# A graph network's update stage: the second tile's normalised rows are turned one step later

## The reference

```python
h = h + (agg.reshape(n, TD) @ wo[l] + bo[l])
xn2 = _layernorm(h, ln2_g[l], ln2_b[l])
ffn = jax.nn.gelu(xn2 @ w1[l] + b1[l], approximate=False) @ w2[l] + b2[l]
h = h + ffn
```

```python
edge_proj = edge_attr @ W_sum + b_sum
sum3d = jax.ops.segment_sum(edge_proj, src, num_segments=num_nodes)
```

## Time and profile before

| | us |
|---|---|
| median of 3 runs | 5238.9 (5233.25 to 5239.08) |
| the profiled execution's own time | 5237.1 |
| its span in the trace | 5235.3 |
| PE busy | 3812.7 (73% of the span) |
| DVE busy | 3650.4 (70%) |
| ACT busy | 2132.3 (41%) |
| POOL busy | 3941.4 (75%) |
| first and last norm of update(0) | 1874.9 and 2516.5 |
| first and last norm of update(1) | 4223.3 and 4973.9 |

### The profile page before, as it was taken

The page is one execution under the profiler, slowest core; times in us unless marked ns, Lnnn a source line. Parts: engine busy times, 40 slices in busy tenths (PEclk is TensorE's granted clock), DMA queues, the critical chain, the costliest instruction groups (busy, mean ns, idle before and its releaser), DMA issues. The chain is left out here.

```text
span 5235.3 us, 86953 instructions
## 1 busy us (share of the span) xinstructions
PE 3812.7 (73%) x17590; PEld 3000.8 (57%) x17591; DVE 3650.4 (70%) x9882; ACT 2132.3 (41%) x5069; POOL 3941.4 (75%) x4715
## 2 busy tenths in 40 slices
PE   1695777777777778888685777777777767777759
PEld 0344555555555567778443555555555557766646
DVE  3696888888888856666474888888888844444458
ACT  0113555555555523333113555555555523333322
POOL 2217888888888647777787888888888658888867
PEclk9898999999999989998896999899999978888879
DMA  3366666667666556666676766677666456666658
GB/s 112 118 201 199 201 199 199 197 197 201 198 196 199 144 129 140 139 130 134 117 156 176 203 197 199 197 196 202 199 198 197 134 128 127 125 123 126 132 142 238
DMA packets 664282, 882.62 MB, mean 169 GB/s; under 512 B 126257, under 2 KB 492269, under 8 KB 664013
## 3 DMA queue, kind: packets, MB, share of 16 engines
q0 software_dynamic: 261248, 529.64, 42.8%
q1 hardware_dynamic: 369907, 322.55, 20.8%
q10 hardware_dynamic: 32860, 28.05, 1.9%
HBM read 749.33 MB, written 130.59 MB: 168 GB/s over the span
## 5 line engine op out<-in xcount | busy, mean ns | idle before, releaser
L859 POOL DMA_INDIRECT kv<-kv_scratch,src_u x1760 | 1687.4, 959 | 364.3 <-POOL spacer L839 189.4
L1130 PE MATMUL sum_p<-msg,hot_s 128*128 128x273 f32 x3520 | 1091.6, 458 | 736.5 <-issue 499.5
L1318 POOL DMA_INDIRECT sum_scratch<-ysum,dest x700 | 1100.9, 1573 | 284.1 <-issue 153.5
L1130 PEld LDWEIGHTS sum_p<-msg,hot_s 128*128 128x128 f32 x3520 | 716.7, 215 | 1024.5 <-issue 697.5
L1118 PE MATMUL qe<-sums,hot_q 128*128 x3520 | 900.6, 401 | 74.5 <-ACT hot_q L890 48.8
L1118 PEld LDWEIGHTS qe<-sums,hot_q 128*128 128x128 f32 x3520 | 715.5, 206 | 216.9 <-issue 84.6
L996 DVE SCALAR_TENSOR_TENSOR sums<-sums,keep,sum_p 128x273 f32 x880 | 434.6, 494 | 436.7 <-PE sum_p L1130 326.5
L899 ACT ACTIVATE hot_s<-iota_f,ndrel_u 128x128 f32<-128x128 f32 x1760 | 559.4, 391 | 307.2 <-PE sum_p L1130 209.5
L970 DVE TENSOR_TENSOR prod<-qe,kv 128x1024 f32<-128x1024 f32 x440 | 535.9, 1218 | 67.5 <-DMA kv<-kv_scratch,src_u 66.4
L839 POOL MEMSET spacer<- 128x384 bf16 x1320 | 573.9, 435 | 0.9
L985 DVE TENSOR_TENSOR msg<-kv,turned 128x1024 f32<-128x1024 f32 x440 | 533.1, 1212 | 44.3 <-issue 34.6
(11 more groups left out here) (247 smaller groups left out, 5237.7 us busy)
## 6 DMA issues: line engine op xcount, KB each, us to landing
drow<-drel_scratch SPq DMA_DIRECT2D x220, 256.0 KB
ea<-in_edge_attr SPq DMA_DIRECT2D x100, 512.0 KB
srow<-in_src_rows SPq DMA_DIRECT2D x100, 512.0 KB
kv<-kv_scratch,src_u POOLq DMA_INDIRECT x1760
kv_scratch<-res SPq DMA_DIRECT2D x100, 256.0 KB
hin<-h_scratch SPq DMA_DIRECT2D x154, 128.0 KB
h_scratch<-res SPq DMA_DIRECT2D x150, 128.0 KB
masks<-mask_scratch SPq DMA_DIRECT2D x110, 128.2 KB
```

What stands on the lines that cost most here:

```text
L859: g.indirect_dma_start(out=kv[:, slot, :], out_offset=None, in_=KVd, in_offset=bass.IndirectOffsetOnAxis(ap=src_u[:, par, u:u + 1], axis=0 ...
L1130: ins = pe.matmul(sum_p[i][:, 0:XW], hot_s[:, q % 2, 2 * i + u, :], msg[:, q % 2, 2 * i + u, :], start=(u == 0), stop=(u == 1))
L1318: g.indirect_dma_start(out=sum_d[r], out_offset=bass.IndirectOffsetOnAxis(ap=dest[:, k, j:j + 1], axis=0), in_=ysum[:, k, j, :], in_offset ...
```

## The change

The norm of the second tile (DVE), its transposes (TensorE) and its copy (ScalarE) leave the end of the turn. In the next turn norm(t, 1) stands behind attention(t + 1, 0), turn_norm(t, 1) behind up(t, 0), and turned_norm(t, 1) behind gelu(t, 0). The first tile's turn_norm(t + 1, 0) and turned_norm(t + 1, 0) change places with the att steps of the second tile, so they stand ahead of them. The steps ahead of the loop and behind it follow from that. POOL's and SyncE's lists are unchanged, and both calls of update() get the same change.

```diff
                        for k in range(2):
                            stats(0, k)
-                        for k in range(2):
-                            norm(0, k)
+                        norm(0, 0)
 
                         def turn(t):
                             attention(t + 1, 0)
+                            norm(t, 1)
                             repeats(t, 0)
                             result(t, 0)
                             stats(t + 1, 0)
...
                             result(t, 1)
                             stats(t + 1, 1)
                             next_moments(t, 1)
-                            norm(t + 1, 1)
 
                         with v.Fori(0, PAIRS - 1) as t:
                             turn(t)
+                        norm(PAIRS - 1, 1)
...
-                        for k in range(2):
-                            turned_norm(0, k)
+                        turned_norm(0, 0)
                         a.wait_ge(prep, 2)
                         with a.Fori(0, PAIRS - 1) as t:
                             gelu(t, 0)
+                            turned_norm(t, 1)
                             turned_att(t + 1, 0)
                             sums_out(t, 0)
                             gelu(t, 1)
+                            turned_norm(t + 1, 0)
                             turned_att(t + 1, 1)
-                            turned_norm(t + 1, 0)
                             sums_out(t, 1)
-                            turned_norm(t + 1, 1)
-                        for k in range(2):
-                            gelu(PAIRS - 1, k)
-                            sums_out(PAIRS - 1, k)
+                        gelu(PAIRS - 1, 0)
+                        turned_norm(PAIRS - 1, 1)
+                        sums_out(PAIRS - 1, 0)
+                        gelu(PAIRS - 1, 1)
+                        sums_out(PAIRS - 1, 1)
...
-                        for k in range(2):
-                            turn_norm(0, k)
+                        turn_norm(0, 0)
                         with pe.Fori(0, PAIRS - 1) as t:
                             up(t, 0)
+                            turn_norm(t, 1)
                             turn_att(t + 1, 0)
                             down(t, 0)
                             out_proj(t + 1, 0)
                             sum_group(t, 0)
                             up(t, 1)
+                            turn_norm(t + 1, 0)
                             turn_att(t + 1, 1)
-                            turn_norm(t + 1, 0)
                             down(t, 1)
                             out_proj(t + 1, 1)
                             sum_group(t, 1)
-                            turn_norm(t + 1, 1)
-                        for k in range(2):
-                            up(PAIRS - 1, k)
-                            down(PAIRS - 1, k)
-                            sum_group(PAIRS - 1, k)
+                        up(PAIRS - 1, 0)
+                        turn_norm(PAIRS - 1, 1)
+                        down(PAIRS - 1, 0)
+                        sum_group(PAIRS - 1, 0)
+                        up(PAIRS - 1, 1)
+                        down(PAIRS - 1, 1)
+                        sum_group(PAIRS - 1, 1)
```

## The result

The changed kernel takes 5251.7 us (median), the kernel before 5239.1 us in the runs beside it. The ratio is 1.0024, with a 95% interval of 1.0015 to 1.0033. So the change costs 12.7 us. That is slower by 0.24%, where 5232 us and a range of 5205 to 5251 us were forecast. Ten of the eleven executions of the changed kernel took 5247 to 5255 us; one took 9206 us, in a slower state of the chip, and stands outside the ratio.

A forecast was written before the change was run, and what follows sets the result against it. Update(0) was taken as bound by POOL's scatter loop and the edge-load loop, update(1) by POOL's queue. Saving 7 us in update(0) and 0 in update(1): 5237.1 - 7 + 1.8 = 5232 us, range 5205 to 5251 us.

The forecast's parts named there:

- what the change does on TensorE: TensorE, update(0): up(t, 0) starts without a wait; idle time moves to turn_norm(t + 1, 0), down(t, 1) behind it 2.0 us longer.
- What the second turn_norm was to keep, about 1 us: TensorE, update(0): idle time left at turn_norm(t, 1), waiting for xn behind up(t, 0), about 1 us.
- POOL is next: POOL, update(0): scatters colliding with loads limit the turn next; landing waits still 60 us or more.
- What is late next: POOL: Update(0): earlier loads collide with POOL's scatters, holding the turn at 26.4 us.
- POOL pays 2.2 us, and the turn is 24.2 + 2.2 = 26.4 us: POOL, update(0): second scatter 6.86 us behind the last one instead of 4.7 us without a wait.
- The saving of 7 us: Update(0): 24 turns at 26.4 us instead of 26.7 us save 7 us; update(1) saves 0.
- The other 2.5 us are mostly one wait: POOL, update(0): the turn's 2.5 us beyond 24.2 us are mostly the second tile's second scatter awaiting the first tile's sixth.
- The load loop is then 26.2 us, level with POOL's 26.3 us: Update(0): load loop of 24.2 us plus 2.0 us for a slow down(t, 1); both loops together give 26.4 us.
- rival (c): Nothing to measure: rs withholds what TensorE stops withholding, DVE's wait changes its name only; 5239 us, chance 0.22.
- rival (b): Update(0): load loop gets free of the collision and sets a 25.2 us turn; 36 us saved, 5203 us, chance 0.17.
- Rival (d): Update(1): cold down(t, 1) makes loads 2 us later, sixth to eighth scatters land late; 16 us slower, 5255 us, chance 0.16.
- DVE's waits for products under 20 us: Sign in update(0): DVE's waits for TensorE's products fall from 68 us to under 20 us.

The follow-up runs named there:

- a_warm: Changed kernel plus 20 filler transposes of the identity on TensorE ahead of turn_norm(t + 1, 0); 5252.3 us, ratio 1.0023 to the kernel before.
- a_rot: Changed kernel with the second tile's scatter tables in update(0) turned by two, (j + 2) % 4; 5211.4 us, ratio 0.9946 to the kernel before.
- b_rot: Kernel before the change with the second tile's scatter tables in update(0) turned by two; 5208.1 us, ratio 0.9934.
- a_loads: Changed kernel with each tile's store and edge loads right behind its own node loads on SyncE; 5273.5 us, ratio 1.0063 to the kernel before.
- a_again: The unedited changed kernel measured a second time; 5252.5 us, ratio 1.0023 to the kernel before.
- only_u1: Kernel before with the changed order in update(1) alone; 5243.7 us, ratio 1.0010.
- only_u0: Kernel before with the changed order in update(0) alone; 5249.6 us, ratio 1.0017.
- a_noswap: Changed kernel with turn_att(t + 1, 1) again ahead of turn_norm(t + 1, 0) on TensorE; 5255.6 us, ratio 1.0030 to the kernel before.
- late loads: Both stores issued ahead of the first edge load on SyncE: in the changed kernel 5235.1 us (0.9992), in the kernel before 5229.0 us (0.9978).
- the same filler: 20 extra transposes ahead of turn_norm(t + 1, 0): in the changed kernel 5252.3 us, in the changed kernel with tables turned by two 5203.5 us.

## Why the prediction was wrong

**Right: what the change does on TensorE.** up(t, 0) starts without a wait. The idle time went to the first tile's turn_norm, 3.11 us within the forecast 2 to 4 us, and made down(t, 1) 1.7 us longer (forecast 2.0 us). What the second turn_norm was to keep, about 1 us, went as well.

The Trainium skill (TensorE: Matmul & The Clock Gate, section HAM oscillation) says that in a loop of matmuls each batch behind a wait for its data starts cold, and the trace of the changed kernel agrees in its steady turns: behind each of the twelve waits of 3.10 to 3.12 us down took 4.5 to 5.3 us. It doesn't in one turn: behind the 3.38 us at 2025.69 us down took 3.62 us. The section gave no price for the kernel, and a_warm measured it: 0.6 us in the wrong direction, within the intervals, as long as POOL sets the turn.

**Right: POOL is next.** The landing waits stayed (68.9 us, at least 60 forecast). The turn hung on the collision of loads and scatters, and a_rot and b_rot show it by taking the waits behind it away.

**Wrong: the size of the collision.** The step that failed is in "What is late next: POOL": "POOL pays 2.2 us, and the turn is 24.2 + 2.2 = 26.4 us". The 2.2 us came from the one turn that began with xn waiting for rs, with a distance of 6.86 us at a place of -1.45 us. The 19 turns of a_warm with a place between -1.38 and -1.34 us average 7.3 us (6.8 to 7.9 us), so that turn was a lucky one. The old kernel's own mean was already 7.09 us, that is 2.4 us paid, and 24.2 + 2.4 = 26.6 us is no gain. The changed kernel's is 7.38 us: 2.7 us paid, 3.1 us in its steady turns. With that, 24.2 + 2.7 = 26.9 us, against 27.0 us measured; this only shows that the sum closes, since the 2.7 us were measured afterwards. The saving of 7 us was the difference of a lucky turn and an average.

The place of the wait was misread, too. "The other 2.5 us are mostly one wait", that of the second scatter, holds for the turn at 2145.00 us. In the turn that gave the 2.2 us the second scatter waited for nothing (0.30 us at 2171.36 us); the first one did:

```profile
2169.47 1.59 POOL L1318 DMA_INDIRECT sum_scratch<-ysum,dest  x1 [2.83 <-DMA sum_scratch<-ysum,dest]
```

With loads ahead of the last scatter the wait stands there, and a_loads, which moved them further ahead, only made it longer.

**Wrong: two loops side by side.** "The load loop is then 26.2 us, level with POOL's 26.3 us" treated the cold down as a price of a second loop that POOL's loop would hide. It is one closed loop: load, landing, second scatter, rs, xn, down, h, load. In the changed kernel's turn that is 7.55 + 9.93 + 7.39 + 2.44 = 27.31 us, from the rows above and h at 2248.50 us. Lengths taken around a turn always add up to it; that the loop is closed is read from the waits along it, for the landing (3.40 us), rs (1.27 us), xn (3.11 us) and down (1.51 us). The cold down and out_proj (1.51 + 0.55 us of DVE's waits) hold the place at +0.26 us, where the distance is longest. Without them the place is -1.35 us and the distance little shorter. So neither order of things gets below the old 26.7 us.

**Missed: that the sign of "no gain" could be negative.** The price of rival (c), "DVE's wait changes its name only", was put at exactly 0. The mechanism held (scol 65.8 to 106.7 us, products 68.3 to 46.6 us). But the new wait isn't worth the old one. Either kernel has four turns with a distance under 6.5 us, all of them at places beyond +0.45 us, among them the turn of 25.2 us on which rival (b) counted. The other twenty average 7.4 us in the old kernel, whose places move between -1.45 and +0.6 us, and 7.8 us in the changed one, which sits where the distance is longest.

**Rival (d)** got the sign and nearly the size (5255 us), but by another way. It put the loss in update(1), whose landing waits are unchanged at 4.6 us and whose loss is 3 to 5 us if it is one. Also wrong was "DVE's waits for products under 20 us": they stayed at 46.6 us, because the cold down brought its own.

**Open.** Why scatters land late beside loads that were issued up to 0.45 us behind them, and whether the loads or the store ahead of them do it, isn't shown. The 12.7 us themselves are not fully resolved either. In POOL's loop between the second rs and the last but one the profile shows 6.3 us more (634.4 against 628.1 us): 3.1 us of landing waits beyond 0.3 us each and 2.8 us of longer scatter instructions. Single executions scatter by half as much: a_again has a mean distance of 7.17 us with the same 27.0 us turn, and in only_u1, where update(0) is the old one, first norm to last took 645.2 us instead of 641.6 us, with a mean distance of 7.35 us. The place is the steadier sign: with the changed order in update(0) (the changed kernel, a_again, only_u0, a_noswap) 16, 16, 18 and 21 of 24 turns lie between -0.15 and +0.45 us, with the old order (the kernel before, only_u1) 2 and 6. And with the rotation, which takes the waits away, the two orders differ by 3.3 us instead of 12.7, about what update(1) may cost. So the shift from 7.09 to 7.38 us fits the loss, but isn't proven as its cause. Only the larger steps, rotation and late loads, are far outside that.

## What to carry to other kernels

Where an engine's wait is removed, ask what then pins the turn, and take the price of that from the mean over all turns, not from the one turn that looks like the new kernel. If the bound is a dependency on a DMA that lands late, lengthen the dependency first, and look at every instruction that has one, not only at the one that waits in the turn shown: turning the tables by two cost nothing and gave 0.66%, while reordering the engines in front of it gave nothing or less. Keep a matmul loop warm only once its own loop sets the turn; the same filler was worth 0 us before the rotation and 7 to 8 us after it.

## What the runs showed of the hardware

- How late a scatter lands depends on where a burst of loads starts against it, and steeply so: a load issued 1 us later (+0.2 to +1.2 us) shortens the distance from 7.8 to 5.3 us.
- Loads issued earlier are not safer. At -1.3 us the distance is still 7.3 us, with the wait at the first scatter (2.45 us) instead of the second, and split into two early bursts they cost 21.7 us more than the changed kernel.
- Scatter instructions themselves vary: 1.60 and 1.68 us in the rows of a_warm, 1.54 us in most others.
- The idle time right ahead of a product doesn't say alone whether it runs slowly. Two turns of a_rot have the same wait for xn, 1.90 us. Behind the one down takes 5.30 us, behind the other 3.62 us. TensorE's timeline of a_rot:

```profile
2201.18 0.44 PE L1577 MATMUL tp<-ident,xn 128*128 128x128 f32 x2 [1.90 <-DVE xn L1409]
...
2201.67 5.30 PE L1597 MATMUL w_p<-w_s,uT 128*128 128x256 f32 x16
...
2226.66 0.44 PE L1577 MATMUL tp<-ident,xn 128*128 128x128 f32 x2 [1.90 <-DVE xn L1409]
...
2227.15 3.62 PE L1597 MATMUL w_p<-w_s,uT 128*128 128x256 f32 x16
```
